# An audio tower on one core: the order tables of TensorE, VectorE, ScalarE and GpSimd replaced

## What is computed

```python
h = layernorm_affine(patches(x) @ tok_W.T + b)                  # 512 -> 256
h = h + attn0(_layernorm(h))      # 16 heads of 64, causal, softcap 50, sigmoid gate per head, w_out
h = h + ffn0(_layernorm(h))       # tanh(((x @ W) @ A1) @ A2 + bias), each 256 x 256
h = h + attn1(_layernorm(h))      # 16 heads of 16, a Fenwick mask of 16 x 16, projection
h = h + ffn1(_layernorm(h))       # fp4 weights and activations, gate and up 256 -> 704, silu, down
def fp4_quant_dequant(x):                                       # blocks of 16 along the last axis
    scale = jnp.maximum(max(abs(xb)) / 6.0, 1e-12)
    return _GRID[jnp.searchsorted(_MID, abs(xb / scale))] * sign(xb) * scale
```

## Time and profile before

| | us |
|---|---|
| median of 3 runs | 336.06 |
| lowest and highest of them | 335.31, 336.49 |
| the profiled execution | 336.39 |
| its span, first to last instruction | 334.5 |
| PE busy in it (matmuls) | 300.7 |
| DVE busy | 244.7 |
| ACT busy | 114.6 |
| POOL busy | 27.9 |

### The profile page before, as it was taken

One profiled execution on the slowest core, in us unless ns is written; L12 is line 12 of the kernel. 1 busy time (PEld: TensorE's weight loads), 2 busy tenths in 40 slices (PEclk: granted clock), 3 DMA queues, 4 the chain that ended last, 5 costly groups with the idle time before them and its releaser, 6 DMA issues.

```text
span 334.5 us, 11728 instructions
## 1 busy us (share of the span) xinstructions
PE 300.7 (90%) x5122; PEld 264.8 (79%) x5122; DVE 244.7 (73%) x527; ACT 114.6 (34%) x259; POOL 27.9 (8%) x49
## 2 busy tenths in 40 slices
...
GB/s 249 347 336 199 1 3 129 4 0 2 4 4 2 68 0 2 2 3 2 4 19 18 4 4 0 2 2 3 20 19 4 2 2 5 2 2 0 0 18 47
DMA packets 8773, 12.80 MB, mean 38 GB/s; under 512 B 778, under 2 KB 5650, under 8 KB 8724
## 3 DMA queue, kind: packets, MB, share of 16 engines
...
...
HBM read 11.01 MB, written 1.05 MB: 36 GB/s over the span
## 4 chain that ended last, share of the span: by engine, by line
PE 79%; DVE 8%; issue 6%; ACT 3%; DMA 2%; POOL 1%; SPq 0%; POOLq 0%; ACTq 0%; DVEq 0%
PE psum L1182 72%; DMA wqkv_raw<-in_L_attn_w_qkv_dram 2%; PE psum L1360 2%; PE psum L1382 1%; PE psum L1485 1%; PE psum L1267 1%; PE psum L1242 1%; POOL ln_rs L539 1%; DVE xT_lo L821 1%; DVE qs L803 1%; PE psum L1462 1%; ACT wqkv_hi L554 0%; SPq L469 0%; DVE ln_st L870 0%; POOLq L218 0%
## 5 line engine op out<-in xcount | busy, mean ns | idle before, releaser
L539 POOL TENSOR_TENSOR ln_rs<-ln_mv,minus_half 128x1 f32<-128x1 f32 x40 | 26.8, 674 | 267.7 <-DVE ln_mv L873 267.6
L1182 PE MATMUL psum<-aT_hi,wqkv_hi 128*128 128x256 f32 x128 | 37.4, 293 | 0.3 <-ACT v_aug L554 0.3
L1182 PE MATMUL psum<-aT_lo,wqkv_hi 128*128 128x256 f32 x128 | 36.0, 281 | 0.0
L1182 PE MATMUL psum<-aT_hi,wqkv_lo 128*128 128x256 f32 x128 | 35.9, 281 | 0.0
L554 ACT ACTIVATE qkT<-psum 128x512 f32<-128x512 f32 x32 | 19.1, 598 | 32.7 <-PE psum L1182 32.7
L1182 PE MATMUL psum<-wout_s,oT 128*128 128x256 f32 x128 | 29.1, 381 | 0.0
L1182 PEld LDWEIGHTS psum<-wout_s,oT 128*128 128x128 f32 x128 | 24.0, 190 | 3.3
L1182 PEld LDWEIGHTS psum<-aT_hi,wqkv_hi 128*128 128x128 f32 x128 | 24.1, 189 | 1.3 <-issue 0.7
L1182 PEld LDWEIGHTS psum<-aT_lo,wqkv_hi 128*128 128x128 f32 x128 | 24.1, 188 | 0.0
L1182 PEld LDWEIGHTS psum<-aT_hi,wqkv_lo 128*128 128x128 f32 x128 | 24.1, 188 | 0.0
L1182 PE MATMUL psum<-bias_parts,pick_r 128*128 128x256 f32 (+1 forms) x40 | 15.4, 385 | 5.7 <-DVE res L901 2.4
...
## 6 DMA issues: line engine op xcount, KB each, us to landing
...
w_raw<-in_L_attn_W_qkv_dram SPq DMA_DIRECT2D x1, 768.0 KB, 10.1
...
```

The lines of the kernel that those rows point to most:

```text
L539: nc.gpsimd.tensor_tensor(ln_rs[:, s, k, j:j + 1], ln_mv[:, s, k, j, 1:2], minus_half[:, :], ALU.pow).then_inc(rstd_ready[f"{k}_{j}"], 1)
L1182: return nc.tensor.matmul(o_, a, b, start=first, stop=last)
```

## The change

Only the lists of the table `ORDER` are different: those of PE, ACT, DVE and POOL. The stages in them are the same, and so are their instructions, shapes and loads; the list of SP is the same. Banks and semaphore counts follow from the lists, so they move as well. A line or two of each list:

```diff
 ORDER = {e: order.split() for e, order in {
     "pe": """
-        turn_tok xT0.0 bcast tok0.0 xT1.0 tok1.0 xT0.1 turn_ff tok0.1 xT1.1 join_ff1 aT.0 tok1.1 v11.0 v00.0
-        v12.0 qk5.0 qk7.0 qk0.0 v10.0 qk6.0 qk1.0 qk2.0 qk3.0 v01.0 v02.0 qk4.0 aT.1 xT0.2 turn_gate0 s0.0
-        join_ff2 s1.0 turn_gate1 qk3.1 qk2.1 mix0.0 qk4.1 qk0.1 oT01.0 mix1.0 v11.1 oT00.0 qk5.1 qk6.1 qk1.1
...
+        turn_tok xT0.0 bcast tok0.0 xT1.0 tok1.0 xT0.1 tok0.1 xT1.1 turn_ff join_ff1 tok1.1 aT.0 v01.0 qk6.0
+        qk2.0 qk3.0 qk1.0 qk5.0 v12.0 qk7.0 v00.0 xT0.2 qk0.0 v02.0 qk4.0 v11.0 v10.0 aT.1 turn_gate1 join_ff2
+        s0.0 turn_gate0 s1.0 qk5.1 mix0.0 qk6.1 v01.1 qk4.1 oT00.0 mix1.0 v11.1 qk3.1 qk1.1 qk7.1 qk2.1 oT01.0
...
     "act": """
-        turn_tok xT0.0 tables split_qkv0 split_qkv2 bcast xT1.0 split_qkv3 split_qkv4 xT0.1 split_b turn_ff
...
+        turn_tok xT0.0 tables split_qkv1 split_qkv2 split_qkv3 bcast xT1.0 split_qkv4 split_qkv5 split_b xT0.1
...
     "dve": """
-        tokB1.0 xT0.1 tokC1.0 split_qkv4 st1_1.0 tokA0.1 xT1.1 tokB0.1 ln1_1.0 w0a aT.0 tokA1.1 tokB1.1
...
+        tokA1.0 tokB1.0 xT0.1 tokC1.0 w0a tokA0.1 st1_1.0 split_qkv5 tokB0.1 xT1.1 ln1_0.0 ln1_1.0 w0b tokA1.1
...
     "pool": """
-        tok0.0 tokln0.0 tok1.0 tokln1.0 tok0.1 tok1.1 tokln1.1 tokln0.1 ln2_0.0 ln3_0.0 ln2_1.0 tok0.2 ln3_1.0
...
+        tok0.0 tokln0.0 tok1.0 tokln1.0 tok0.1 tok1.1 tokln1.1 tokln0.1 ln2_0.0 ln2_1.0 ln3_0.0 tok0.2 ln3_1.0
```

133 lines of the change are left out of this document (66 added, 67 removed).

## The result

| | before | after |
|---|---|---|
| median | 335.32 us (20 runs) | 337.45 us (20 runs) |
| lowest and highest | 332.65, 340.91 | 335.12, 339.2 |
| ratio, with its 95% interval | | 1.0073 (1.0048 to 1.0097) |
| profiled execution | 336.39 us, span 334.5 | 338.44 us, span 336.6 |

The change makes the kernel slower by 0.7%, 2.4 us; by the medians and by the two profiled executions it is 2.1 us. The forecast was +2.7 us. The single runs of one kernel differ by up to 2.5%, and the longer ones have the lower mean granted clock: in 23 runs of the kernel before it was 0.960 to 0.995.

What follows compares the result with a forecast made beforehand. PE bounds the kernel, with stalls at the ends of instruction pieces, and DVE the end. Terms 2.3 + 0.2 + 3.7 + 1.2 - 3.5 + 0.8 - 2.0 = +2.7 us gave 338.8 by the median; range 331.0 to 341.0.

Steps and rivals of the forecast that it cites:

- start: Up to the first projection of aT.0: it starts at 31.2 instead of 28.93 us, +2.3 us, bounds 0 to 4.
- projections of pass 0: PE's projections in pass 0: some present waits go, new ones for split_b and a bank come, +0.2 us, bounds -1 to +2.
- around join_ff2, with the clock: Near join_ff2 and s1.0: an instruction piece delayed by w_out, +3.7 us, and the clock drop behind its stall, +1.2 us.
- 62 to 97 us: PE from 62 to 97 us: most of its 3.77 us idle goes, -3.5 us, bounds -3.8 to -1.
- 97 to 267 us: Middle: 4.0 us of idle and clock goes, nine short pieces and closer waits come, +0.8 us, bounds -3 to +3.
- tail: End, set by DVE: ten fewer instructions after mx1_1.3, 4.1 us, less PE's 2.2 us delay, -2.0 us, bounds -4 to 0.
- The held piece: Inside s1.0, after 78 of 128 matmuls: PE's next instruction piece is held up by w_out's load, stall 4.65 us.
- it starts 5.2 us and is usable 7.6 us after that issue: Timing of the instruction piece near join_ff2's end, counted from SP's issue of w_out; gave the 4.65 us stall.
- no instruction packet until w_out is through: Sign to look for near 58 us: no instruction packet runs until w_out's load has finished.
- The clock: Behind the new stall in s1.0: one drop of the granted clock, among dense projections, +1.2 us.
- The rival "not held": Near join_ff2: w_out does not hold up the piece, 1.1 instead of 4.65 us and no clock drop; 334.0, chance 0.25.
- the rule of 3.5: All along PE: a piece of 256 instructions that PE could execute in under 3.5 us costs the difference.

Runs made afterwards that it cites:

- the hold: Changed kernel, but SP issues the 1 MB load of w_out only when qk5.1 is done; against the kernel before: 333.53 us, 0.9942.
- the shifted kernel: Kernel before with 64 instructions that only wait put ahead of turn_tok on PE, no work moved: 349.01 us, 1.0395 of the kernel before.
- The last five kernels: Changed kernel with the old start lists, three variants of w_out issue and s0.0 order: 1.0006, 1.0002, 1.0037; first two with turn_gate1 earlier on DVE: 1.0027, 1.0024.

## Why the prediction was right

The forecast was +2.7 us, 338.8 by the median, in a range of 331.0 to 341.0; measured were +2.4 us by the ratio (+2.1 by the medians) and 337.45. Term by term, by the table of the result:

| term | forecast | measured in the profile | |
|---|---|---|---|
| start | +2.3 | +2.8 | right; 31.8 us for 31.2 |
| projections of pass 0 | +0.2 | +0.2 | right |
| around join_ff2, with the clock | +4.9 | +3.6 | mechanism right, split wrong |
| 62 to 97 us | -3.5 | -3.3 | right |
| 97 to 267 us | +0.8 | +0.1 | within its bounds |
| tail | -2.0 | -1.4 | right |
| sum | +2.7 | +2.05 | |

*The held piece.* The place (78 of 128), the cause (w_out, shown by the hold) and the fall of the clock were right. The stall was put at 4.65 us and was 2.08: the step that failed is "it starts 5.2 us and is usable 7.6 us after that issue". It started 3.35 us after the issue and was usable 5.65 us after it. One case of before was taken for a fixed delay; "no instruction packet until w_out is through" was wrong with it, since 461 of w_out's 1040 packets started behind the piece's. That makes 1.95 us of the error; the other 0.6 is that PE was through with its own piece 3.57 us after the issue and not 3.0, as turn_gate0 waited 0.69 us for DVE. The clock, put at 1.2 us, cost more: it stayed at 0.50 for over 6 us and not for 3, and PE fell back by 2.6 us between the starts of qk5.1 and mix1.0. The two errors nearly cancel, and that the sum comes out so near is luck to this extent. The rival "not held", 334.0, is what the hold made of the kernel: 333.5.

*The middle.* Seven pieces that had 2.85 to 3.47 us of work by the count lasted 3.49 to 3.93 us, as the rule of 3.5 said; one with 2.81 us took 2.88 us. The idle time put down to their ends is 2.0 us of the 3.6 that were forecast. But the held kernel has the same order, and there the piece that took 3.54 us with a stall of 0.50 (its end is at 212.82 us) took 2.89 us and had none: its transfer started 0.55 us after PE had entered it, and 1.33 us in the changed kernel. So 3.5 us is a mean over such delays and not what each piece needs, and the term of the middle rests on it. Two slips of the prediction change little: the stall of 0.58 us has the last 6 matmuls of mx1_1.3 behind it, not of val1_1.3, and 132 matmuls in 17.89 us make 1.6 us for 12 of them, not 1.5.

*The tail.* DVE's timeline before, `den1_1.3` and the last step of `hh_1.3`:

```profile
289.68 0.26 DVE L1084 RECIPROCAL den1b<-psum 128x16 f32<-128x16 f32 x1 [0.31 <-PE psum L1182]
...
325.90 0.89 DVE L817 TENSOR_TENSOR hhb<-hhb,qs 128x704 f32<-128x704 f32 x1
```

After:

```profile
295.35 0.25 DVE L1084 RECIPROCAL den1b<-psum 128x16 f32<-128x16 f32 x1
...
327.65 0.89 DVE L817 TENSOR_TENSOR hhb<-hhb,qs 128x704 f32<-128x704 f32 x1
```

DVE's way between them fell from 37.1 to 33.2 us, 3.9 us, as forecast (4.1); PE's extra work ahead of mx1_1.3 (2.1 us, forecast 2.2) took half of it back. So this term was right in its parts and not only in its sum.

*The rule's flaw.* The piece that PE entered at 289.34 had 4.0 us of work and stalled all the same, in PE's timeline of the kernel after:

```profile
294.52 0.37 PE L1182 MATMUL psum<-v_b,k1sb 32*32 32x17 f32 x21 [1.16 <-issue]
```

Its transfer starts only at 292.17. The same shows in most pieces of the changed kernel that begin with large matmuls (the transfer starts 2.4 to 4.9 us after PE enters them) against those that begin with the small ones (mostly 0.6 to 1.6 us). So the transfer seems not to be asked for at the entry, as the prediction had it, but when some tens of instructions of the piece are through (20 to 80 of them when it starts, in those pieces), and from its start 2.2 to 2.9 us pass until PE goes on. A slow head and a fast rest stall, whatever the piece's sum. That may also be why the stalls of the shifted kernel grew by twice what the rule gave; no run tests it apart.

*The start as a term of its own.* Its size was right, and its meaning was not. The last five kernels show that an earlier start is lost again at DVE near 50 to 60 us under the new order. In a sum of terms along the program, the later one holds only for the earlier one as it is.

Which part of the net loss is the start's is therefore open: no kernel here has the changed middle with DVE's steps placed for an early start.
